# A convolution and spiral-scan kernel: in the scan, TensorE adds a tile's sums before it hands over the tile four ahead

## The reference, cut to what matters

```
def step(g, inp):
    ci, ni, nm, nc = inp
    local = g[:, ci, :]
    nb = g[:, ni, :]
    neigh = (nb * nm[None, :, None]).sum(axis=1) / nc
    u = jnp.concatenate([local, neigh], axis=-1)
    y_sc = jnp.tanh(u @ w1 + b1) @ w2 + b2
    g = g.at[:, ci, :].set(local + y_sc[:, None] * w_y[None, :])
    return (g, None)
```

## Time and profile before

| | |
|---|---|
| median of 3 runs | 4929.23 us (4926.02 to 4929.77) |
| the profiled execution's own time | 4930.04 us |
| its span in the trace | 4928.2 us |
| TensorE busy | 4550.9 us (92%) |
| VectorE busy | 4011.7 us (81%) |
| GpSimd busy | 3477.0 us (71%) |
| ScalarE busy | 2521.4 us (51%) |
| DMA over the span | 835.36 MB, mean 170 GB/s |
| scan (first hand-over to the end) | 3195.5 us to the end |

### The profile page before, as it was taken

How to read it: one execution, slowest core, us unless ns; L and a number is a source line. 1 busy time by engine, 2 the same in 40 slices (tenths; PEclk the granted TensorE clock), 3 DMA queues, 4 the chain that set the end, 5 groups by cost and what they waited for, 6 DMA issues and landing times.

```text
span 4928.2 us, 62800 instructions
## 1 busy us (share of the span) xinstructions
PE 4550.9 (92%) x19641; PEld 3326.0 (67%) x19641; DVE 4011.7 (81%) x6107; ACT 2521.4 (51%) x4454; POOL 3477.0 (71%) x2478
## 2 busy tenths in 40 slices
PE   3999999999999999999999999888888888887888
PEld 2788878888888888888888888644444444444445
DVE  5888888888887888888888888288888888877753
ACT  3566655666566666666666665343444443333321
POOL 3888888888887888888888888556666655554332
PEclk7999999999999999999999999999999999999999
DMA  3344444444444444444444442499999988876531
GB/s 93 115 132 140 131 139 131 140 130 140 130 140 132 136 131 140 131 139 131 140 131 139 132 138 105 167 312 298 294 312 295 286 272 253 248 228 196 173 125 37
DMA packets 395143, 835.36 MB, mean 170 GB/s; under 512 B 76865, under 2 KB 178497, under 8 KB 394689
## 3 DMA queue, kind: packets, MB, share of 16 engines
q1 hardware_dynamic: 251408, 420.08, 31.3%
q0 software_dynamic: 143408, 411.26, 22.3%
HBM read 419.95 MB, written 425.85 MB: 172 GB/s over the span
## 4 chain that ended last, share of the span: by engine, by line
PE 70%; ACT 10%; DVE 9%; issue 8%; DMA 2%; POOL 1%; SPq 0%; DVEq 0%; POOLq 0%; ACTq 0%
PE psum L846 12%; PE psum L848 12%; PE psum L847 12%; PE psum L830 12%; PE psum L859 9%; DVE psum L704 4%; ACT relu_rows L531 4%; PE psum L819 3%; PE psum L868 3%; PE psum L878 2%; PE psum L880 2%; ACT u_hi L554 2%; ACT psum L549 2%; DMA out<-dw_rows 1%; PE psum L879 1%
## 5 line engine op out<-in xcount | busy, mean ns | idle before, releaser
L629 DVE SCALAR_TENSOR_TENSOR dw_rows<-relu_rows,taps,dw_rows 128x1792 f32<-128x1792 f32 x872 | 1804.2, 2080 | 25.4 <-ACT dw_rows L520 20.3
L451 POOL DMA_INDIRECT s_pre<-eo,wave_idx x784 | 1361.0, 1736 | 248.7 <-issue 220.6
L464 POOL DMA_INDIRECT out<-dw_rows x897 | 892.0, 994 | 839.4 <-DVE dw_rows L712 603.8
L445 POOL DMA_INDIRECT s_x<-xo,wave_idx x784 | 1202.1, 1533 | 319.3 <-issue 229.5
L846 PE MATMUL psum<-w_hi,u_hi 128*128 128x512 f32 x3136 | 1382.4, 441 | 0.0
L848 PE MATMUL psum<-w_hi,u_lo 128*128 128x512 f32 x3136 | 1231.1, 393 | 0.0
L847 PE MATMUL psum<-w_lo,u_hi 128*128 128x512 f32 x3136 | 1223.6, 390 | 0.0
L859 PE MATMUL psum<-dw_rows,ident 128*128 128x512 f32 x1794 | 961.2, 618 | 161.4 <-DVE near L704 155.0
L485 ACT ACTIVATE eo<-psum 128x512 f32<-128x512 f32 x784 | 468.1, 597 | 1217.5 <-PE psum L848 1137.2
L549 ACT ACTIVATE psum<-psum 128x512 f32<-128x512 f32 x897 | 522.1, 582 | 907.3 <-PE psum L868 907.3
L830 PE MATMUL psum<-pw,dw_rows 128*128 128x256 f32 x3136 | 819.2, 384 | 62.7 <-ACT psum L540 58.1
(11 more groups left out here) (90 smaller groups left out, 4034.9 us busy)
## 6 DMA issues: line engine op xcount, KB each, us to landing
dw_rows<-s_pre SPq DMA_DIRECT2D x615, 256.0 KB
x_tok<-x SPq DMA_DIRECT2D x112, 896.0 KB, 6.8
dw_rows<-s_x SPq DMA_DIRECT2D x615, 128.0 KB
dw_rows<-s_pre SPq DMA_DIRECT2D x169, 192.0 KB
dw_rows<-s_x SPq DMA_DIRECT2D x169, 96.0 KB
out<-dw_rows POOLq DMA_INDIRECT x897
s_x<-xo,wave_idx POOLq DMA_INDIRECT x784, 3.2
s_pre<-eo,wave_idx POOLq DMA_INDIRECT x784, 3.7
```

What stands on the lines that cost most here:

```text
L445: pool.indirect_dma_start(s_x, bass.IndirectOffsetOnAxis(wave_idx[:, n:n + 1], 0), xo[:, n % XO_SLOTS, :], None, bounds_check=TILES * P - ...
L451: pool.indirect_dma_start(s_pre, bass.IndirectOffsetOnAxis(wave_idx[:, n:n + 1], 0), eo[:, n % EO_SLOTS, :], None, bounds_check=TILES * P - 1,
L464: pool.indirect_dma_start(out_rows, bass.IndirectOffsetOnAxis(store_idx[:, c:c + 1], 0), o_t[:, c % OUT_SLOTS, :], None, bounds_check=OUT_ ...
L629: dve.scalar_tensor_tensor(out=dst, in0=pair_rows(relu_rows, k + ky - 1, c, 2 * kx * NB), scalar=taps[:, c, 3 * ky + kx:3 * ky + kx + 1], ...
```

## The change

Two statements change places in TensorE's loop over the tiles. No instruction is added or taken away, and no wait is changed.

```
             for c in range(AHEAD):
                 hand_over(c)
             for c in range(TILES):
+                add_sums(c)
                 if c + AHEAD < TILES:
                     hand_over(c + AHEAD)
-                add_sums(c)
                 alone = live(SEQ[c][0]) == 1
                 if alone:
                     idle_products(8)
```

## The result

The change makes the kernel slower: 4944.35 us, median of 7 runs (4937.99 to 4951.96), against 4930.92 of before (7 runs, 4926.02 to 4936.35). The ratio is 1.0027, 95% interval 1.0016 to 1.0038. I had forecast 4922 and a range to 4943. The profiled execution took 4937.99, the fastest of the seven, with a span of 4936.2 us.

A forecast was written before the change was run, and what follows sets the result against it. In the scan no engine is full, so a ring of waits sets each level's time, with DMA near its limit at 7 and 6 groups. Terms 27.5 + 8.5 - 3.5 + 2 - 10 - 21 - 11 = -7.5 us gave 4922, range 4902 to 4943.

The forecast's parts named there:

- 3 groups: 3-group levels: a second hand-over stands ahead of part 1's turn; 6.21 becomes 7.07 us, +27.5 us over 32 levels.
- 4 groups: 4-group levels: a half takes 3.79 against 3.66 us with both hand-overs ahead of the turn, +8.5 us over 64 halves.
- 2 groups: 2-group levels: about even, TensorE's new ring 2.71 us against VectorE's bound of 2.68, +2 us over 64.
- 5 groups: 5-group levels: long half 0.25 us shorter, short half 0.13 longer, -0.12 x 32 levels, given as -3.5 us.
- 1 group: 1-group levels: the hand-over moves to where TensorE had time; 4.80 becomes 4.43 us, -10 us over 28 levels.
- eight idle products of 0.213 to 3.25 ... So it just fits: 1-group levels: hand-over until 1.55, idle products until 3.25 us after L768, with the turn wanted at 3.23.
- the rival that I gave 0.12: Idle products delay the 1-group turn: 0.03 us longer each makes it 0.25 late, gain 2 or 3 us, time 4930; chance 0.12.
- 7 and 6 groups: 7- and 6-group levels: faster by what the DMA lets through, -21 and -11 us, bounds 0 and 0 to -40 and -16.
- The rings: 7- and 6-group levels: wait chains shorten from 11.38 to 10.13 and 9.56 to 9.06 us, at most -40 and -16 us.
- I take -0.65 per level with 7 groups: 7-group gain sized by DMA rate, between 0.48 (97% share, average rate) and 1.12 us (332 GB/s), nearer the first.
- the wait moves to the stores and loads: Rival: 7- and 6-group levels stay at 11.4 to 11.5 and 9.7 us, held by store waits; time 4954, chance 0.16.
- the first rival: The DMA does not bind in 7- and 6-group levels; the rings' full -56 us come, time 4898; chance 0.17.

The follow-up runs named there:

- e7_idle6: The changed kernel with 6 idle products in place of 8 ahead of the turn in 1-group levels; ratio 1.0020 to the kernel before, that stage 138.3 us.
- e8_slots8_light: The changed kernel with 8 output slots in place of 4 and only 32 rows of each s_x tile loaded (a probe); ratio 0.9920 to the kernel before.
- e12_only76: The kernel before with the change in the 7- and 6-group levels alone, the old order elsewhere; ratio 0.9959 to the kernel before.
- e10_slots8_again: The changed kernel with 8 output slots in place of 4, run again on another chip; ratio 1.0039 to the kernel before.

## Why the prediction was wrong

**3 groups, +27.5 forecast, +27.4 measured.** Right by its own steps, to 0.01 us per level.

**4 groups, +8.5 and +8.1. 2 groups, +2 and -0.5** (2.70 per half, 2.71 worked out; the last level of the stage gives that back, 7.13 in place of 7.81). **5 groups, -3.5 and -5.7**: 8.34 per level against the 8.32 worked out (-0.12 x 32 is -3.8, not -3.5); the rest are fewer slow levels.

**1 group, -10 and -5.6.** The step that failed: "eight idle products of 0.213 to 3.25 ... So it just fits". No run shows 0.213. In the trace of before eight weight loads of L886 take 1.81 us, the last of them 0.19, so they start 0.231 apart, and so do the products after the change: 0.14 us more for eight. The turn came 0.12 us late; this is the small form of the rival that I gave 0.12, and e7_idle6 shows it: with six the stage gives the whole 10.0.

**7 and 6 groups, -21 and -11 forecast, -13.0 and -5.3 measured.** This is the term that was mis-sized, by 14 us. The rings were right (e8_slots8_light: 10.20 and 9.10 per level, 10.13 and 9.06 worked out). What was wrong is how I sized what the DMA lets through: "I take -0.65 per level with 7 groups", between 0.48 and 1.12, and -0.35 with 6. I set the rate of the DMA engines as the limit, and named the stores' slots beside it without a price. The runs show the slots in its place. With 8 of them 16 levels in a row took 9.11 us at a share of 0.98, where I had 9.38 from the rate. In the changed kernel it is the slots that are seen waiting: L712's waits for stores go from 7.0 to 18.7 us over 300 us, and the DMA share only from 0.93 to 0.95. The measured gain per 7-group level, 0.41, lies under the lower of my two numbers, 0.48, and the 0.17 of the 6-group levels is half of my 0.35. What the rate would do to the 7-group levels by itself isn't settled, since with 8 slots the stalls take them over. The rival "the wait moves to the stores and loads" had the mechanism, at a part of its price.

With these terms as measured, 27.4 + 8.1 - 5.7 - 0.5 - 5.6 - 13.0 - 5.3 = +5.4: the sign turns. The terms of 3, 4, 5 and 2 groups came to +29.3 (forecast +34.5); against them I had 42 us of gains, and 23.9 came. So the sign hung on the term that had the widest bounds. The medians of the timed runs are 13.4 apart, another 8 us: 2.6 of the two profiled executions lie ahead of the scan, and that of the change was the fastest of seven. Timed runs of the change spread over 14 us, those of before over 10. The stages of the slower runs are not on record; that the 7-group order took up to 6.4 us more in four other executions says where a part may lie. Without these 8 us the time would have stood inside my range: that the sign came out clear of noise is not explained by the mis-sized term alone.

The rule that I weighed, about 358 GB/s in the Trainium skill, DMA: Bandwidth & Descriptors, section Specifications, would have left the DMA unbound: the first rival. The runs here stay under that figure: 312 GB/s at a share of 0.95 in the changed kernel, 330 to 332 over 146 us at 0.98 to 0.99 with 8 slots. For the 6-group levels the first rival was nearer than I was: once no store was waited for, they ran at the ring's time.

## What to carry to other kernels

When work is moved within one engine's queue, follow the ring of waits in each stage by itself: the same 0.86 us was on the ring in one stage, hidden in another, and gave time back in a third, and the terms cancelled in the total. With each stage in the order that suits it, 1.1% came. Where a ring gets shorter, price every buffer that it turns over (slots x time per tile against the latency of a store), not only the rate of the engines behind it: the fuller engines cost nothing in 16 levels with 8 slots, and 4 slots cost 26.1 us. Run a control on the same chip as what it controls. And a sum of large terms of both signs is as uncertain as its worst term: the forecast of its sign should say so.

## What the runs showed of the hardware that I had not expected

The 16 DMA engines kept a share of 0.98 and 330 GB/s for 146 us without making the 6-group levels longer. With 8 slots and full load the 7-group levels have stalls in which what TensorE's products release comes up to 5.4 us late, and the granted clock drops to the lower of its two levels behind them, 0.96 on average over the stretch. What they wait for stays open. The chip is one rival: the three kernels with many stalls ran on two chips on which every kernel has one or more, and none of those on the other chips has any. The recording is another: on the same two chips the traces hold only 444 to 502 of the 897 signals of L868, on the others all of them. The 8 slots are part of it: e12_only76, with the same order in these levels and 4 slots, has one late turn in the whole scan where e10_slots8_again has 16 on the same chip. Whether they do it by the fuller load is not told apart. And the untouched first part of the program took between 3197.8 and 3231.1 us to the first dot from one execution to the next, more than the whole effect of this change.
